# Four attention layers: turned scores ahead of scores in each half step, a first pair of batches by itself, one empty step, loads in another order

## The chip, the cores and the metric

The kernel runs on one core of one Trainium2 chip, in a single launch. The metric is the device time in microseconds of that core, taken over several executions; one more execution is profiled. Its engines are TensorE (PE, with PEld for its weight loads), VectorE (DVE), ScalarE (ACT), GpSimd (POOL) and SyncE (SP), which here only issues DMAs.

## The reference

Four layers of cross attention run one after the other on x of 8 batches x 128 tokens x 128 features, with a context of the same shape. Each has 16 heads.

```python
# L0: heads of 8; a padding mask on the keys; then LayerNorm with gamma, beta
x = LN(x + softmax(q(x) k(ctx) / sqrt(8) + mask) v(ctx) wo + bo)
# L1: heads of 64; RMS norm of x ahead, no scale
x = x + softmax(q(rms(x)) k(ctx)) v(ctx) wo
# L2: block of three
x = x + self_attn(LN(x))      # heads of 8, causal, blocks of 64 dropped by a router
x = x + cross_attn(LN(x), ctx)  # heads of 8, biases
x = x + relu(LN(x) f1 + b) f2 + b   # 512 hidden
# L3: heads of 8, with biases; LayerNorm with gamma, beta at the end
x = LN(x + softmax(q(x) k(ctx) / sqrt(8)) v(ctx) wo + bo)
```

## The kernel before, in words

**Items and steps.** Attention with heads of 8 is done four times over 8 batches: L0, L2 (the self attention), LC (the cross attention of the same block) and L3. That makes 32 items n = 0 to 31, one batch of one layer each. L1, with heads of 64, has a loop of its own (`pe_l1`, `act_l1`, `dve_l1`) between items 7 and 8, and fills about 94 to 202 us. The other items go through a software pipeline of steps s, one item entering per step (`pe_attn`, `act_attn`, `dve_attn`, `pool_attn`). `at(s)` (L200) gives the item of a step. Between LC and L3 there are `HOLES` = 2 steps (24 and 25) into which no item enters, since L3 needs the result of the feed-forward layer, which is itself computed in steps 22 to 30 between attention work. So item 24 enters at step 26, and the last at step 33.

**A step.** It has two halves, for heads with even and odd number of a pair. In half 0 of step s TensorE does, in `pe_scores` (L288): the scores S of item s, queries on the partitions, into banks 0 and 1 (L294); the turned scores T of item s-2 in its second half, keys on the partitions, into banks 4 and 5 (L302); the causal matmuls of L2 (L306, L311); the transpose of the split maxima of item s-1 (`pe_mT`, L326); and the max rows (L320), which add the negative row maximum to the turned scores. Then come the extras of the step (`even(s)`), the transposes `pe_back` (L353) and the output projection `pe_z` (L362). In half 1 it does S of item s for banks 2 and 3, T of item s-1 for its first half, the max rows, `pe_onT` (L358), the extras `odd(s)` and `pe_V` (L345). The instructions of an engine run in the order written, each behind its waits.

**The chain of an item.** S -> VectorE's max of each half (`dve_max`, L465) -> GpSimd splits the 16 maxima into three bf16 parts (`pool_split`, L443 to L448) -> transpose on TensorE, bank 3 -> ScalarE copies it (`act_mrow`, L387) -> T and max rows -> ScalarE's exp (`act_exp`, L393), straight from the turned scores -> V on TensorE -> `act_osum` (L400) -> back -> `dve_norm` (L481, L485) -> onT -> z -> `dve_z` (L493). S of the next item needs its banks free: they are free when max has read them, and when whatever an extra has put there since has been read. `FREED` and `S_ready` hold these waits; the waits for the data of a pair of batches are there too (`data_of_S`).

**Stacks.** Scores are computed to full precision by splitting q and k into three bf16 parts: p0 by ScalarE (`act_p0`, L620), the rest by VectorE (`dve_rest`, L639; L0's k first by `dve_raw`, L599, which applies the mask), p1 by ScalarE (`act_p1`, L647), p2 by VectorE or GpSimd (`any_p2`, L651). DMAs stack the parts into `qs`, `ks0`, `ks1` (`stack_dma`, L663): six for q and six for k of a group of batches, three with p0 and p1, p2 behind. They are issued by SyncE in one order for all layers, except the first q pair of L0, which ScalarE issues. L0's mask goes as three bf16 parts through `up`, a transpose and `kaug` into rows of `ks0`.

**Other work between.** L1's V products for all batches (`pe_v1`, 16 chunks of 512 columns, L705, copied by ScalarE, L710) and the transposes of its weights (`pe_a1`) are extras of L0's steps; `free` waits until max has read the bank. Extras of the later steps: turns of the normalised x (`pe_turn`, L564, copied by `act_turn`, L569) under the names T1, T2, TC, TF, T3, projections (`pe_proj`, L578), V of a layer (`pe_v`, L672), the feed-forward layer (`pe_f1` L927, `pe_f2` L950, `dve_ff` L958). In L3's query part of step s = 24, 26, 28, 30: projection in the even half (bank 2, second half), p0 there, the rest at the end of VectorE's even half, p1 in ScalarE's odd half, p2 on VectorE at step s+1, scores at step s+2.

**The loads.** SyncE issues at the start the first weights, the context in two halves and the mask in two halves, then waits for ks0's zeros (one memset of 128 x 4096 on VectorE, L1465, ahead of everything else on that engine), then the stacks of L0, and only then x, the row vectors `wrow` and the large weights (L988 to L992). `pool_resid` (L523) of L0 adds a bias to x; it stands in GpSimd's queue at step 2, behind split(1) and vpad and ahead of split(2) (L1048).

## Time and profile before

| | us |
|---|---|
| median of 3 executions | 412.18 |
| lowest, highest | 406.12, 413.94 |
| the profiled execution | 406.76 |
| its span, first to last instruction | 405.0 |
| PE, DVE, ACT, POOL busy | 318.9, 248.4, 213.3, 98.8 |
| mean granted TensorE clock, 1 is full speed | 0.928 |

The profile gives times in us from the start of the span. In a line of the timeline the first number is the start, the second the time until the end of the group, then engine, line, operation, output<-input, shape and the number of instructions; in brackets the idle time of the engine before it and what ended it. SPq and ACTq are DMA issues. A window's line gives its length, then for each engine the busy time and in brackets the instructions, then the granted TensorE clock, the share of the DMA engines' time and GB/s.

### The profile page before, as it was taken

What the parts mean: (1) busy time and instruction counts of PE and PEld (TensorE: products, weight loads), DVE (VectorE), ACT (ScalarE), POOL (GpSimd) and SP (SyncE); (2) the same over time, 40 slices, a digit from 0 to 9 for tenths busy, and PEclk for the clock granted to TensorE, in tenths of its full rate; (3) what the DMA queues carried; (4) which work ended last, traced back from release to release, by engine and by line L of the source; (5) the groups of instructions that cost most, each with busy time, mean ns of one, the idle gap of its engine ahead of it and who ended that gap; (6) DMA issues with size and microseconds to landing.
All of it is one profiled execution on the core that took longest, in us unless ns stands there. A gap on an engine that the chain in (4) does not pass through costs nothing.

```text
span 405.0 us, 10131 instructions
## 1 busy us (share of the span) xinstructions
PE 318.9 (79%) x4045; PEld 225.1 (56%) x4045; DVE 248.4 (61%) x482; ACT 213.3 (53%) x457; POOL 98.8 (24%) x268
## 2 busy tenths in 40 slices
PE   5378099898899999798777986886887977797882
PEld 2134055676687778667654543564555664575551
DVE  6445026844997565658656675678757555446864
ACT  1536046676676786678534543445555542335560
POOL 6011323330020001003238213322423321312311
PEclk9979659999999999999999998999989996679998
DMA  6343920000000000002311132202321011010000
GB/s 228 94 116 92 346 104 4 2 3 0 2 2 3 0 2 0 2 2 73 85 41 42 45 99 62 73 21 59 85 82 34 2 41 32 8 34 28 23 28 26
DMA packets 26068, 20.49 MB, mean 51 GB/s; under 512 B 3182, under 2 KB 24566, under 8 KB 25766
## 3 DMA queue, kind: packets, MB, share of 16 engines
q1 hardware_dynamic: 24566, 18.27, 15.1%
q10 hardware_dynamic: 1456, 1.58, 1.1%
q8 instruction: 32, 0.52, 0.5%
q14 instruction: 14, 0.11, 0.1%
HBM read 6.63 MB, written 0.52 MB: 18 GB/s over the span
## 4 chain that ended last, share of the span: by engine, by line
PE 48%; ACT 16%; DVE 14%; issue 9%; POOL 4%; SPq 3%; DMA 3%; ACTq 1%; POOLq 0%; DVEq 0%
ACT probs L832 5%; PE psum L294 4%; PE psum L345 4%; PE psum L320 4%; PE psum L705 4%; PE psum L756 4%; PE psum L731 3%; PE psum L790 3%; SPq L663 3%; ACT probs L840 3%; PE psum L302 3%; PE psum L927 3%; PE psum L950 2%; DVE maxs L465 2%; PE psum L767 2%
## 5 line engine op out<-in xcount | busy, mean ns | idle before, releaser
L465 DVE TENSOR_REDUCE maxs<-psum 128x8 f32<-128x1024 f32 x64 | 77.7, 1216 | 49.0 <-PE psum L294 34.5
L393 ACT ACTIVATE probs<-psum 128x1024 f32<-128x1024 f32 x64 | 65.5, 1023 | 48.5 <-PE psum L320 46.7
L294 PE MATMUL psum<-ks,qs 64*128 64x128 bf16 x512 | 27.2, 229 | 37.1 <-DVE rest L639 10.1
L294 PEld LDWEIGHTS psum<-ks,qs 64*128 64x128 bf16 x512 | 16.7, 98 | 54.4 <-issue 49.6
L345 PE MATMUL psum<-probs,vpad 128*32 128x128 f32 x1024 | 37.0, 288 | 0.0
L832 ACT ACTIVATE probs<-psum,maxs 128x128 f32<-128x128 f32 x128 | 34.8, 391 | 0.5 <-DVE maxs L880 0.5
L345 PEld LDWEIGHTS psum<-probs,vpad 128*32 128x32 f32 x1024 | 27.8, 115 | 13.1 <-issue 9.5
L387 ACT COPY mrow<-psum 128x128 bf16<-128x128 bf16 x32 | 8.5, 265 | 46.4 <-PE psum L326 43.1
L536 POOL TENSOR_SCALAR rstd<-stats 128x2 f32<-128x2 f32 (+1 forms) x19 | 5.2, 273 | 111.4 <-DVE stats L501 111.2
L443 POOL CAST mp<-maxs 128x16 bf16<-128x16 f32 x32 | 6.9, 215 | 93.3 <-DVE maxs L465 92.6
L302 PE MATMUL psum<-qs,ks 64*128 64x128 bf16 x512 | 26.7, 223 | 2.5 <-ACT probs L393 2.5
L880 DVE TENSOR_REDUCE maxs<-psum 128x8 f32<-128x1024 f32 x16 | 19.5, 1221 | 13.7 <-PE psum L756 13.7
L890 DVE TENSOR_REDUCE mres<-probs 128x8 f32<-128x1024 f32 x16 | 19.4, 1215 | 12.3 <-ACT probs L832 12.3
L320 PE MATMUL psum<-mrow,sel 32*128 32x128 bf16 x512 | 26.6, 225 | 0.0
L481 DVE RECIPROCAL rsum<-psum 128x16 f32<-128x16 f32 x32 | 8.1, 255 | 28.8 <-PE psum L353 28.6
L302 PEld LDWEIGHTS psum<-qs,ks 64*128 64x128 bf16 x512 | 17.9, 98 | 5.3 <-ACT probs L393 4.3
L705 PE MATMUL psum<-wmat,ctxT 128*128 128x512 f32 x32 | 20.2, 734 | 0.9 <-DVE maxs L465 0.9
L320 PEld LDWEIGHTS psum<-mrow,sel 32*128 32x128 bf16 x512 | 15.1, 96 | 10.0 <-issue 5.7
L840 ACT COPY probs<-psum 128x1024 f32<-128x1024 f32 x16 | 16.7, 1042 | 7.0 <-PE psum L767 7.0
L782 PE MATMUL psum<-probs,v1all 128*64 128x128 f32 x256 | 17.5, 279 | 3.3 <-ACT probs L840 2.9
L400 ACT COPY osum<-psum 128x256 f32<-128x256 f32 x32 | 12.0, 375 | 15.1 <-PE psum L345 14.4
L894 DVE TENSOR_TENSOR probs<-probs,mres 128x1024 f32<-128x1024 f32 x16 | 19.6, 1225 | 0.6
(159 smaller groups left out, 663.1 us busy)
## 6 DMA issues: line engine op xcount, KB each, us to landing
qs<-part_q SPq DMA_DIRECT2D x78, 64.0 KB, 2.0
ks<-part_k SPq DMA_DIRECT2D x30, 128.0 KB, 2.4
ks<-part_k SPq DMA_DIRECT2D x36, 64.0 KB, 2.0
wmat<-in_wmat SPq DMA_DIRECT2D x1, 1856.0 KB, 11.5
wmat<-in_wmat SPq DMA_DIRECT2D x1, 1024.0 KB, 7.3
qs<-part_q SPq DMA_DIRECT2D x6, 128.0 KB, 2.4
wrow<-in_wrow SPq DMA_DIRECT2D x1, 704.0 KB, 5.0
ctxT<-in_ctxt SPq DMA_DIRECT2D x2, 256.0 KB, 5.4
```

The source lines that it names most:

```text
L294: s_mm = e.matmul(bank(2 * half + r)[:, bt(c)], qs[rows, i, bt(b)], ks[L.slot][rows, i, bt(b)], start=(c == 0), stop=L is not L2, skip_gro ...
L302: e.matmul(bank(4 + r)[:, bt(c)], ks[M.slot][rows, i, bt(b)], qs[rows, i, bt(b)], start=(c == 0), stop=False, skip_group_check=True)
L320: mm = e.matmul(bank(4 + a)[:, bt(i)], sel[rg(j), i, :], mrow[rg(j), m % 2, :], start=False, stop=True, skip_group_check=True)
L345: mm = e.matmul(o_bank(n)[rg(c), bt(half)], vpad[:, n % 2, 4 * half + c, G * a:G * a + G], pt, start=(a == 0), stop=(a == 1), skip_group_c ...
L393: e.activation(probs_of(n, half), bank(4, 2), ACT.Exp, scale=layer(n).scale)\
L465: e.tensor_reduce(maxs[:, n % 2, 8 * half:8 * half + 8], bank(2 * half, 2).rearrange("p (h k) -> p h k", k=P), AX.X, ALU.max, negate=True)\
L705: e.matmul(bank(to), ctxT[:, bt(c // 2)], mat("v1")[:, c % 2 * 512:(c % 2 + 1) * 512], start=True, stop=True).then_inc(L1("v_mm"), 1)
L832: ins = e.activation(probs[:, half, bt(s)], bank(2 * half, 2)[:, bt(s)], ACT.Exp, bias=maxs[:, b % 2, 8 * half + s:8 * half + s + 1])
L840: e.copy(pT[:, half, :], bank(4, 2)).then_inc(L1("pT_out"), 1)
L880: e.tensor_reduce(maxs[:, b % 2, 8 * half:8 * half + 8], bank(2 * half, 2).rearrange("p (h k) -> p h k", k=P), AX.X, ALU.max, negate=True)\
L890: e.tensor_reduce(sums, p8, AX.X, ALU.add).then_inc(L1("sum"), 1)
L894: e.tensor_tensor(p8, p8, rec.unsqueeze(2).broadcast_to([P, 8, P]), ALU.mult).then_inc(L1("norm"), 1)
```

## The change

- `HOLES` is 1: item 24 enters at step 25, and everything behind is one step earlier (steps end at 36, outputs at 31, 33, 35, 37, GpSimd's rstd at 30 to 36).
- `pe_scores` puts T and the max rows of its item ahead of S of the other item, in each half. The transpose of the split maxima comes behind both. ScalarE's `act_mrow` comes behind the exp of the second half.
- The projections of L0 are done for batches 0 and 1 first, then 2 and 3, then 4 to 7. The loads of context, mask and x are cut at 2 batches, not 4.
- ks0's zeros are made by three engines: GpSimd a quarter behind qs's, ScalarE a quarter (an activation with scale 0), VectorE a half behind the parts of the mask. kaug is copied by VectorE, not ScalarE, and stacked by one DMA of 128 rows, not three of 16.
- ScalarE does p0 and p1 of the first pair and then issues all six q transfers in a row. V of L0 for batches 4 to 7 moves from step 1 to ahead of step 0; one v1 chunk fewer is made ahead of step 0, and step 2 has two in its odd half.
- x and wrow are issued behind the q stack of batches 2 and 3, ahead of the stacks of batches 4 to 7. L0's `pool_resid` is at step 3.
- `rest` gets a whole buffer for k.
- End of L1: the turn and the projections of T2's batches 4 and 5 go behind the scores of item 8, their p0 and rest behind the end of L1, their p2 behind GpSimd's split at step 9. T2's first turn is one place later.
- LC's p1 and p2 of q go to the head of the step on their engines. L3's p1 goes to ScalarE's even half and its p2 to the end of VectorE's even half of the same step; L3's projection takes the first half of bank 2 and TF's turn the second half of bank 3, in front of the transpose of the maxima.

```diff
-HOLES = 2
+HOLES = 1
...
-        V1_EVEN = {1: (4,), 2: (7,), 3: (9,), 4: (11,), 5: (13,), 6: (15,)}
-        V1_ODD = {0: (2, 3), 1: (5, 6), 2: (8,), 3: (10,), 4: (12,), 5: (14,)}
-        freed(0, 1, sem("v_out_L1"), 2)
+        V1_EVEN = {1: (3,), 2: (6,), 3: (9,), 4: (11,), 5: (13,), 6: (15,)}
+        V1_ODD = {0: (1, 2), 1: (4, 5), 2: (7, 8), 3: (10,), 4: (12,), 5: (14,)}
+        freed(0, 1, sem("v_out_L1"), 1)
...
-        def pe_scores(e, n, half, m, mhalf, turned=None):
-
-            if n is not None:
-                L, b = layer(n), n % B
-                S_ready(e, n, half)
-                for c, r, rows, i in heads(half):
-                    s_mm = e.matmul(bank(2 * half + r)[:, bt(c)], qs[rows, i, bt(b)], ks[L.slot][rows, i, bt(b)],
-                                    start=(c == 0), stop=L is not L2, skip_group_check=True)
-                if L is not L2:
-                    s_mm.then_inc(sem("S_mm"), 1)
+        def pe_scores(e, n, half, m, mhalf):
+
             if m is not None:
                 M, b = layer(m), m % B
                 T_ready(e, m, mhalf)
                 for c, r, rows, i in heads(mhalf):
                     e.matmul(bank(4 + r)[:, bt(c)], ks[M.slot][rows, i, bt(b)], qs[rows, i, bt(b)],
                              start=(c == 0), stop=False, skip_group_check=True)
-            if n is not None and L is L2:
-                for j in (2 * half, 2 * half + 1):
-                    s_mm = e.matmul(bank(j), identB[:, :], causal[:, 0, :].unsqueeze(1).broadcast_to([P, 4, P]),
-                                    start=False, stop=True, skip_group_check=True)
-                s_mm.then_inc(sem("S_mm"), 1)
-            if m is not None and M is L2 and mhalf:
-                for a in range(2):
-                    e.matmul(bank(4 + a), causal[:, 0, :], identB[:, :].unsqueeze(1).broadcast_to([P, 4, P]),
-                             start=False, stop=False, skip_group_check=True)
-            if turned is not None:
-                pe_mT(e, turned)
-            if m is not None:
+                if M is L2 and mhalf:
+                    for a in range(2):
+                        e.matmul(bank(4 + a), causal[:, 0, :], identB[:, :].unsqueeze(1).broadcast_to([P, 4, P]),
+                                 start=False, stop=False, skip_group_check=True)
                 e.wait_ge(sem("mT_read"), m + 1)
                 for i in range(4):
                     for a in range(2):
@@ -320,6 +305,17 @@
                         mm = e.matmul(bank(4 + a)[:, bt(i)], sel[rg(j), i, :], mrow[rg(j), m % 2, :],
                                       start=False, stop=True, skip_group_check=True)
                 mm.then_inc(sem("T_mm"), 1)
+            if n is not None:
+                L, b = layer(n), n % B
+                S_ready(e, n, half)
+                for c, r, rows, i in heads(half):
+                    s_mm = e.matmul(bank(2 * half + r)[:, bt(c)], qs[rows, i, bt(b)], ks[L.slot][rows, i, bt(b)],
+                                    start=(c == 0), stop=L is not L2, skip_group_check=True)
+                if L is L2:
+                    for j in (2 * half, 2 * half + 1):
+                        s_mm = e.matmul(bank(j), identB[:, :], causal[:, 0, :].unsqueeze(1).broadcast_to([P, 4, P]),
+                                        start=False, stop=True, skip_group_check=True)
+                s_mm.then_inc(sem("S_mm"), 1)
...
-        def pe_attn(e, steps, lo, hi, even, odd):
+        def pe_attn(e, steps, lo, hi, even, odd, ahead=lambda s: None):
             for s in steps:
                 n, n1, n2 = at(s, lo, hi), at(s - 1, lo, hi), at(s - 2, lo, hi)
                 n3, n4 = at(s - 3, lo, hi), at(s - 4, lo, hi)
-                pe_scores(e, n, 0, n2, 1, n1)
+                pe_scores(e, n, 0, n2, 1)
+                ahead(s)
+                if n1 is not None:
+                    pe_mT(e, n1)
...
-        def act_attn(e, steps, lo, hi, even, odd):
+        def act_attn(e, steps, lo, hi, even, odd, first=lambda s, half: None):
             for s in steps:
                 n1, n2, n3 = at(s - 1, lo, hi), at(s - 2, lo, hi), at(s - 3, lo, hi)
                 if n3 is not None:
                     act_osum(e, n3)
+                first(s, 0)
+                if n2 is not None:
+                    act_exp(e, n2, 1)
                 if n1 is not None:
                     act_mrow(e, n1)
-                if n2 is not None:
-                    act_exp(e, n2, 1)
                 even(s)
...
-            e.dma_start(ctxT[:, 0:HALF], ctxt_d[:, 0:HALF]).then_inc(sem("in_ctx0"), 16)
-            e.dma_start(maskbc[:, 0:HALF], mask_d[0:HALF].partition_broadcast(P)).then_inc(sem("in_mask0"), 16)
-            e.dma_start(ctxT[:, HALF:T], ctxt_d[:, HALF:T]).then_inc(sem("in_ctx1"), 16)
-            e.dma_start(maskbc[:, HALF:T], mask_d[HALF:T].partition_broadcast(P)).then_inc(sem("in_mask1"), 16)
-            e.wait_ge(sem("ks0_zero"), 1)
-            stack_dma(e, L0, "k", 0, 2, 0)
-            stack_dma(e, L0, "k", 0, 2, 1)
+            e.dma_start(ctxT[:, 0:PAIR], ctxt_d[:, 0:PAIR]).then_inc(sem("in_ctx0"), 16)
+            e.dma_start(maskbc[:, 0:PAIR], mask_d[0:PAIR].partition_broadcast(P)).then_inc(sem("in_mask0"), 16)
+            e.dma_start(ctxT[:, PAIR:T], ctxt_d[:, PAIR:T]).then_inc(sem("in_ctx1"), 16)
+            e.dma_start(maskbc[:, PAIR:T], mask_d[PAIR:T].partition_broadcast(P)).then_inc(sem("in_mask1"), 16)
+            e.wait_ge(sem("ks0_zero"), 3)
+            stack_up(e, L0, "k", 0, 2)
             e.wait_ge(sem("kaug_out"), 1)
-            for k in range(3):
-                e.dma_start(ks0[8 * k + ROW_SLOT::HD, :, :], kaug[G // 2 * k:G // 2 * k + G // 2, :])\
-                 .then_inc(sem("kaug_in"), 16)
-            stack_dma(e, L0, "k", 0, 2, 2)
+            e.dma_start(ks0[ROW_SLOT::8, :, :], kaug[:, :]).then_inc(sem("kaug_in"), 16)
             stack_up(e, L0, "k", 2, 2)
             stack_up(e, L0, "q", 2, 2)
+            e.dma_start(x[:, :, :], x_d).then_inc(sem("in_x"), 16)
+            e.dma_start(wrow[:, :], wrow_d.partition_broadcast(P)).then_inc(sem("in_rows"), 16)
             stack_up(e, L0, "k", 4, 4)
             stack_up(e, L0, "q", 4, 4)
             e.dma_start(wcol[:, :], wcol_d).then_inc(sem("in_cols"), 16)
...
+            e.memset(wide_f32(ks0, 3), 0.0).then_inc(sem("ks0_zero"), 1)
...
-                if s == 2:
+                if s == 3:
                     e.wait_ge(sem("in_rows"), 16)
...
-                if (b, place) == (7, 0):
-                    e.wait_ge(*L2.v_done("v_out", 0))
-                    pe_turn(e, "T2", 4, 2, 7)
                 if (b, place) == (7, 2):
                     e.wait_ge(sem("masks"), 7)
                     pe_scores(e, B, 0, None, 0)
+                    e.wait_ge(*L2.v_done("v_out", 0))
+                    pe_turn(e, "T2", 4, 2, 7)
+                if (b, place) == (7, 4):
+                    pe_scores(e, B, 1, None, 0)
                     e.wait_ge(sem("xnT_T2"), 2)
                     pe_proj(e, L2, "k", 4, 2, 7)
                     pe_proj(e, L2, "q", 4, 2, 7, PAIR)
-                if (b, place) == (7, 4):
-                    pe_scores(e, B, 1, None, 0)
...
-                if 22 <= s <= 28 and s % 2 == 0:
-                    free(e, s, 0)
-                    if s == 24:
-                        e.wait_ge(sem("ff_read"), 1)
-                    pe_turn(e, "TF", s - 22, 2, 2)
                 if 24 <= s <= 30 and s % 2 == 0:
                     p = (s - 24) // 2
                     free(e, s, 0)
                     e.wait_ge(sem("ff_read"), p + 1)
                     e.wait_ge(sem("xnT_T3"), p + 1)
-                    pe_proj(e, L3, "q", 2 * p, 2, 2, PAIR)
+                    pe_proj(e, L3, "q", 2 * p, 2, 2)
 
...
+            def ahead2(s):
+                if 22 <= s <= 28 and s % 2 == 0:
+                    free(e, s, 0)
+                    pe_turn(e, "TF", s - 22, 2, 3, c0=2)
...
-            act_p0(e, L0, "k", 0, 4)
-            act_p0(e, L0, "q", 0, 4, 1)
+            e.wait_ge(sem("identF"), 1)
+            e.activation(wide_f32(ks0, 2), identF[:, 0:1].broadcast_to([P, T]), ACT.Identity, scale=0.0)\
+             .then_inc(sem("ks0_zero"), 1)
+            act_p0(e, L0, "k", 0, 2)
+            act_p0(e, L0, "q", 0, 2, 1)
+            act_p1(e, L0, "k", 0, 2)
+            act_p1(e, L0, "q", 0, 2)
             e.wait_ge(sem("qs_one"), 1)
             stack_dma(e, L0, "q", 0, 2, 0)
-            act_p1(e, L0, "k", 0, 2)
-            act_p1(e, L0, "q", 0, 2)
             stack_dma(e, L0, "q", 0, 2, 1)
-            e.wait_ge(sem("kaug_mm"), 1)
-            e.copy(kaug[:, :], bank(3).bitcast(BF16)).then_inc(sem("kaug_out"), 1)
             stack_dma(e, L0, "q", 0, 2, 2)
+            act_p0(e, L0, "k", 2, 2)
+            act_p0(e, L0, "q", 2, 2, 6)
             act_p1(e, L0, "k", 2, 2)
             act_p1(e, L0, "q", 2, 2)
-            act_v(e, L0, 0, 4)
             act_p0(e, L0, "k", 4, 4)
-            act_p0(e, L0, "q", 4, 4, 6)
-            act_v1(e, 0, 7)
-            act_v1(e, 1, 2)
+            act_p0(e, L0, "q", 4, 4, 7)
+            act_v1(e, 0, 2)
+            act_v(e, L0, 0, 5)
+            act_v(e, L0, 1, 6)
...
+            def first2(s, half):
+                if half == 0 and 15 <= s <= 21 and s % 2:
+                    act_p1(e, LC, "q", s - 15, 2)
+                if half and 24 <= s <= 30 and s % 2 == 0:
+                    act_p1(e, L3, "q", s - 24, 2)
...
+            e.memset(ks0[:, 0:4, :].rearrange("p c t -> p (c t)").bitcast(F32), 0.0).then_inc(sem("ks0_zero"), 1)
+            dve_raw(e, 0, 2, 0)
+            dve_rest(e, L0, "k", 0, 2)
+            dve_rest(e, L0, "q", 0, 2, 1)
             any_p2(e, L0, "k", 0, 2)
             any_p2(e, L0, "q", 0, 2)
+            e.wait_ge(sem("kaug_mm"), 1)
+            e.tensor_copy(kaug[:, :], bank(3).bitcast(BF16)).then_inc(sem("kaug_out"), 1)
+            dve_raw(e, 2, 2, 5)
...
+            def first2(s):
+                if 15 <= s <= 21 and s % 2:
+                    any_p2(e, LC, "q", s - 15, 2)
+
             def end_of_even(s):
                 if 24 <= s <= 30 and s % 2 == 0:
-                    e.wait_ge(sem("xnT_TF"), min(4, (s - 22) // 2 + 1))
-                    dve_rest(e, L3, "q", s - 24, 2, 2, PAIR)
-
-            for s in range(9, 39):
-                dve_attn(e, [s], B, N_ITEM, even2, odd2, end_of_even)
+                    dve_rest(e, L3, "q", s - 24, 2, 2)
+                    any_p2(e, L3, "q", s - 24, 2)
+
+            for s in range(9, 38):
+                dve_attn(e, [s], B, N_ITEM, even2, odd2, first2, end_of_even)
```

## Rows read from the trace of the kernel before

**Rows 1.** Windows of the span; each engine busy, its instructions, then clock, DMA, GB/s
```profile
39.60:59.30 19.70, 9.45 (x95) 5.03 (x92) 3.00 (x4) 4.02 (x7) 5.17 (x12) 0.58 0.65 240
59.30:83.10 23.80, 22.13 (x376) 15.32 (x372) 17.95 (x45) 16.36 (x30) 10.03 (x30) 0.99 0.01 3
247.00:307.40 60.40, 48.03 (x762) 32.38 (x764) 42.04 (x81) 30.21 (x57) 17.30 (x53) 0.92 0.25 69
320.20:387.80 67.60, 54.80 (x792) 39.79 (x788) 39.23 (x83) 30.36 (x61) 17.45 (x56) 0.85 0.10 27
326.80:332.00 5.20, 4.63 (x75) 3.88 (x71) 1.88 (x7) 1.94 (x4) 0.60 (x2) 1.00 0.11 29
332.00:342.80 10.80, 6.44 (x39) 4.11 (x35) 6.29 (x12) 2.70 (x7) 2.77 (x8) 0.71 0.11 30
...
202.00:214.00 12.00, 9.74 (x119) 6.40 (x113) 5.55 (x11) 3.86 (x9) 4.95 (x11) 1.00 0.19 51
```

**Rows 2.** Waits between 32 and 62 us: total us, times, longest
```profile
POOL resid L523 <- DMA wrow<-in_wrow: 13.7, 1, 13.7
```

**Rows 3.** Timeline, 32 to 62 us
```profile
36.63 3.82 SPq L663 DMA_DIRECT2D qs<-part_q  x6
...
39.65 0.40 PE L294 MATMUL psum<-ks,qs 64*128 64x128 bf16 x8
...
41.63 0.43 SPq L990 DMA_DIRECT2D wrow<-in_wrow  x1
...
46.73 2.48 POOL L523 TENSOR_TENSOR resid<-x,wrow 128x512 f32<-128x512 f32 x2 [13.66 <-DMA wrow<-in_wrow]
...
59.27 0.61 PE L294 MATMUL psum<-ks,qs 64*128 64x128 bf16 x8
```

**Rows 4.** Timeline, 0 to 32 us
```profile
1.86 3.51 POOL L1032 MEMSET qs<- 128x4096 f32 x1
...
5.56 1.38 POOL L1034 MEMSET vpad<- 128x1536 f32 x1
5.83 1.50 DVE L1478 CAST probs<-mu 128x128 bf16<-128x128 f32 x1
...
7.05 0.20 POOL L1037 MEMSET causal<- 128x128 bf16 x1
...
7.58 0.23 DVE L1482 CAST probs<-mu 128x128 bf16<-128x128 f32 x1
...
8.19 0.68 DVE L599 TENSOR_TENSOR rest<-psum,xn 128x512 f32<-128x512 f32 x1
...
8.96 1.28 ACT L620 ACT_TABLE_LOAD   x1 [8.96 <-DVE rest L599]
...
20.78 1.04 PE L294 MATMUL psum<-ks,qs 64*128 64x128 bf16 x16 [6.61 <-DMA ks<-part_k]
...
22.75 3.81 SPq L663 DMA_DIRECT2D qs<-part_q  x6
```

**Rows 5.** Groups of instructions by line, 200 to 405 us
```profile
L294 PE MATMUL psum<-ks,qs 64*128 64x128 bf16 x384 | 20.2, 226 | 25.4 <-DVE rest L639 10.1 <-ACT xnT L569 7.7 <-DMA qs<-part_q 2.6
L302 PE MATMUL psum<-qs,ks 64*128 64x128 bf16 x384 | 19.9, 223 | 2.5 <-ACT probs L393 2.5
```

**Rows 6.** Timeline of TensorE, 297 to 298 us
```profile
297.25 0.40 PE L302 MATMUL psum<-qs,ks 64*128 64x128 bf16 x8
...
297.91 0.33 PE L358 MATMUL psum<-identF,onorm 128*128 128x128 f32 x1
```

**Rows 7.** Timeline, 320 to 377 us; last, a row of the page's DMA issues
```profile
321.99 0.66 PE L578 MATMUL psum<-xnT,wmat 128*64 128x256 f32 x4
...
322.69 0.47 ACT L620 ACTIVATE part_q<-psum,bcol 128x256 bf16<-128x256 f32 x1
...
370.29 6.13 SPq L663 DMA_DIRECT2D qs<-part_q  x6
...
qs<-part_q SPq DMA_DIRECT2D x78, 64.0 KB, 2.0
```

158 lines of the change are left out of this document (75 added, 83 removed).

## The prediction

> **What bounds the kernel now.** I read first the busy times by stretch [rows 1], then the waits inside the stretch that stood out [rows 2], then the timeline there [rows 3], the timeline of the beginning [rows 4], and last what TensorE waits for before a group of scores [rows 5, 6] and the way from the L3 query projection to the stacks [rows 7]. The reader is to see four things.
>
> First, TensorE is busy 22.1 of 23.8 us in steps 4 to 7 (59.3 to 83.1), and only 9.5 of 19.7 us in step 3 (39.6 to 59.3), where its granted clock is 0.58 [rows 1]. That step is a hole: GpSimd sits 13.7 us before `pool_resid` until `wrow` has landed, and TensorE with it, since the split of the maxima stands behind the residual in GpSimd's queue [rows 2, 3]. Second, the first scores start at 20.78, released by the last k stack; until then only projections ran [rows 4]. Third, from step 10 on TensorE is not the bound: it is busy 48.0 of 60.4 us (247 to 307.4), and it sits idle before 28 of the 48 groups of scores (counted in the waits by line), 25.4 us in all, mostly until a bank of PSUM is read out (rest 10.1, xnT 7.7) [rows 1, 5]. Behind each of these scores stand the turned scores, which could run. Fourth, between 93.8 and 202 lies L1, which is hardly touched.
>
> **The change part by part.** The profiled execution took 406.76 us, 405.0 of it the span; terms are against that.
>
> *Loads in another order (x and wrow, and `pool_resid` at step 3).* In before, SyncE issues x and then wrow (41.63) behind all twelve (4,4) stack transfers, and they are there at 46.73 [rows 3]; the residual then takes 2.48 us. In after both are issued right behind the q stack of (2,2), whose last issue was at 22.75 + 3.81 = 26.6 in before. 5.1 us from wrow's issue to its use makes some 32, and step 3 starts at 39.65 before [rows 3, 4]. The transfers moved past are the (4,4) stacks: their p0 parts queue behind 1.2 MB, some 5 us, but their last parts wait for VectorE's p2 of step 2 anyway and are not later; the last issue ended at 36.63 + 3.82 = 40.45, with 2.0 to land [rows 7] 42.5, and step 4 would start at about 45.6 [rows 3]. At step 3 the 2.48 us of residual lie between vpad(2) and split(3); max(3,1) ends some 4.5 us into the step, so the maxima hide them with one memset (0.95). If this cover went, 2 us would be lost once. Step 3 took 59.27 - 39.65 = 19.62; steps 4 to 7 take 23.8 / 4 = 5.95. Gain **13.7** (11 to 14).
>
> *First pair by itself.* Half-size operations: VectorE's raw product 0.68 becomes some 0.4, and so on down the chain, twice on ScalarE and three times on VectorE, together about 1.3; the table load of 1.28 leaves the path, since ScalarE now zeroes a quarter of ks0 before the data come [rows 4]; kaug takes one issue for three, some 1.2 less by 0.64 each [rows 3]. ks0's memset goes from the head of VectorE's queue to behind the mask's parts and is halved; GpSimd's of the same size takes 3.51, so 1.75 are left. Against it stand three things. ScalarE issues all six q transfers (0.64 each, 3.8 us [rows 3]) before p0 of (2,2), so (2,2) and (4,4) come later on it, and scores (0,1) now wait for the copy of v1 chunk 0 behind them. And the cast of the mask part: it took 1.50 us where the same cast later took 0.23; it started at 5.83 and ended at 7.33, when GpSimd's run of memsets (5.56 to 7.25) had ended [rows 4]. In after the mask arrives at about 2.7, in the middle of the 3.51 us memset, and GpSimd's run is a quarter of that longer (to 8.1): if the cast waits for all of it, the mask's parts end at 9.1, the memset at 10.9 and the raw product at 11.3, later than the 8.87 of now. ScalarE then has 10.5 us in its queue before scores (0,1) are free (p0 and p1 of the pair 1.8, the issues 3.8, p0 and p1 of (2,2) with their rests in between 1.9, p0 of (4,4) behind VectorE 2.4, the v1 copy 0.6): 21.8, and their maxima end within 0.3 of now; with what goes behind them step 1 starts some 0.8 earlier. If the cast doesn't wait, VectorE is 4 us earlier, ScalarE's issues take back a little, and step 1 starts 4.6 earlier. I take **1** for the start, near the waiting end because of the row of 1.50; the ends are a loss of 1 and a gain of 4.6.
>
> The row shows more than one instruction's hold: the cast, begun beside the vpad memset (5.56 to 6.94), ended 0.39 us after it, with the short ones that followed [rows 4]. The Trainium skill (SBUF — State Buffer, "Who interferes with whom") says that VectorE's cast in a two-port mode and any GpSimd instruction exclude each other on a shared pair of ports, and that whichever starts first has it for its one instruction. By that rule the cast would get in behind the first memset, at 5.4 (1.86 + 3.51) and not at 8.1, and the start would gain 1 + 2.7 = 3.7; by the row it gains 1. No row shows a cast that got in between two memsets.
>
> In steps 1 and 2 a V product (1.11) leaves step 1 and half a v1 pair (0.9) enters step 2: nothing.
>
> *Turned scores first.* Turned scores and max rows together hold TensorE for 0.66 (297.25 to 297.91) [rows 6]. Where scores waited, up to 0.66 now goes under the wait: 28 waits of 0.9 on average [rows 5] give at most 18 us from step 10 on, and less where one is shorter; about 15. What limits it: where VectorE or ScalarE is what the scores wait for, the step gains only the 0.2 by which exp starts earlier, and scores that did not wait come 0.66 later, and with them max (1.22), split (0.95), the transpose and the max rows of the next step. So I take **6** of 15, between -2 (loss) and 11; p1 and p2 of LC's queries, now at the head of ScalarE's and VectorE's step, take away part of the waits for q stacks and are in it. In steps 3 to 8 TensorE idles 0.33 before each group behind a v1 copy and is otherwise full, so I take **3** (0 to 5).
>
> *End of L1.* T2's turn and the (4,2) projections go behind the scores of batch 8, so L1's last two turns no longer stand behind them, and max(8,1) no longer waits for two rests; the projections then stand before scores (9,0). GpSimd loses the two p2 in front of split(8), which the transpose waits for. TensorE is idle 2.3 of the 12.0 us of 202 to 214 [rows 1], and that is the upper end, since none of its work goes. I take **1.5**, since both waits named lie there; -0.5 is the lower end, the projections (about 1 us) half uncovered. The (4,2) stacks come some 5 us later and are needed at step 12, 20 us on.
>
> *One empty step.* The step 326.8 to 332 (5.2 us) goes, but it holds 4.6 us of TensorE's work [rows 1], which moves into its neighbours; of these, step 26 (332 to 342.8) has 4.4 us of idle TensorE, and the pure last steps become one fewer. Without a new wait this would be 5. The new wait: L3's queries had two steps from projection to scores, and have one. From the projection's start (321.99) to the end of p0 (323.16) it is 1.2 us, six issues take 3.8 [rows 3] and the landing 2.0: 7.0 [rows 7]. In a step of 7.5 the projection starts some 1.8 in and the scores stand 0.4 behind the next step's start: 6.1 after it. So some 1 us is waited at steps 25, 27, 29, 31, with f2 and the transposes behind them in TensorE's queue, 4 in all; VectorE also waits for p1 before p2 and its max, but no longer for xnT. Net **1** (-5 to 5).
>
> Sum: 13.7 + 1 + 6 + 3 + 1.5 + 1 = 26.2, so 380.6 at the profiled level. The three timed executions had a median of 412.18, 5.4 above the profiled one; their spread (406.1 to 413.9) is mostly not tied to a stage I can name, and fewer idle stretches should leave less of it. I put half, 2.7, on top: **383**.
>
> **The rivals.**
> 1. *The order gives nothing*: turned scores in front only delay max, split and the max rows by what they fill. For: S, max, split, transpose, max rows are one chain through every step; against: 25.4 us of idle before scores [rows 5]. Without 9 us: 392.
> 2. *The start gains nearly all*: the cast gets the ports as soon as GpSimd's first memset has ended, and the beginning is 3.7 to 4.6 shorter, not 1. For: a cast beside a later GpSimd instruction took 0.23; against: the 1.50. 380. By the rule of the Trainium skill quoted above it is this case.
> 3. *L3's queries come late*: six issues took 6.13 once instead of 3.8 [rows 7], which makes 9.3 of 7.0 and four waits of 3.3 instead of 1; with what stands behind them 10 us more, 393.
> 4. *The load stall stays*, moved to step 3's split, because x and wrow land only beside the stacks: 14 lost, 397.
 It decides once over 76% of that stretch (29 of 38) is at the low level; before, 332 to 342.8 was at 0.71, and it rose again.
>
> **How the numbers follow.** Forecast 0.58, rivals 0.17, 0.13, 0.06, 0.03, 0.03. The range 371 to 398 takes in the ends of the order (11 instead of 6, 5 instead of 3) and the start on one side, rivals 1, 3 and 4 on the other. A measurement tells about 2% (8.2 us) from no change: faster means under 404. Every case but the last is under that; with 0.04 for several ends together, 0.93 faster, 0.04 within, 0.03 slower.
>
> **What would show it.** Right: no wait for wrow on GpSimd, step 3 near 6 us at full clock, a granted clock above 0.928 on the whole; idle before scores from step 10 well under 25.4; idle before turned scores (2.5 now [rows 5]) up by less than that fell. The cast near 5 us if held. DMA waits of 1 to 1.5 before scores at steps 25 to 31. Wrong: steps 4 to 7 still at 5.95, steps 14 to 21 still at 7.5, a hole anywhere between 15 and 60, or 10 us of waits for qs stacks.

## The result and the profile after

The changed kernel took 365.09 us, the median of four executions (362.0 to 367.26), beside 410.75 (406.12 to 413.94) for the kernel before on the same chip: a ratio of 0.892 (95% interval 0.880 to 0.903). Forecast were 383 us and a range of 371 to 398: the direction was right, but the time lies 6 us below the range, a gain of 45.7 us where 29 were forecast. Ratios and their intervals leave out executions more than 1.5% above the fastest of their kernel, medians do not. The profiled execution took 362.0 us, 360.3 of it the span, at a granted clock of 0.98 (before 0.928).

Below, "exp 8.0" is the start of ScalarE's exp of item 8's first half, "exp 7.1" of item 7's second half, and so on; every item has both in every kernel, so a distance between two exps compares a stretch over kernels. The windows of the changed kernel that answer to [rows 1]; the columns are PE, PEld, DVE, ACT, POOL busy with their instructions, then clock, DMA, GB/s:

```profile
36.70:42.50 5.80, 5.80 (x106) 3.32 (x99) 3.00 (x4) 3.92 (x8) 4.27 (x8) 1.00 0.67 190
42.50:65.40 22.90, 22.56 (x389) 15.01 (x388) 17.66 (x44) 16.78 (x31) 10.11 (x31) 1.00 0.28 114
191.19:348.39 157.20, 137.07 (x2240) 92.38 (x2237) 114.26 (x227) 86.45 (x167) 57.14 (x162) 0.98 0.19 52
```

The same stretch as the last row, exp 8.0 to exp 31.1, in the kernel before:

```profile
214.10:393.13 179.03, 144.58 (x2230) 99.86 (x2229) 114.56 (x225) 87.20 (x167) 53.46 (x157) 0.91 0.16 44
```

Step 3 is no hole any more: TensorE is busy in all of the 5.80 us of its window, where it was busy 9.5 of 19.7 [rows 1]. In steps 4 to 7 it is idle 0.3 us, where it was 1.7. The surprise is the last pair of rows: 157.20 us instead of 179.03, so 21.8 us came from where 7 were forecast. The profiled execution was the fastest of its four; in the other profile of the same kernel (`after_again`, below) this stretch took 161.5 us at a clock of 0.95, so two executions of one kernel can differ by some 4 us in such a stretch. TensorE's idle time fell from 34.5 to 20.1 us (14.3), and its busy time from 144.6 to 137.1 (7.5), with the same work and a clock of 0.98 instead of 0.91.

The residual [rows 3] no longer waits. The beginning, in the timeline of the changed kernel:

```profile
1.86 3.51 POOL L1033 MEMSET qs<- 128x4096 f32 x1
3.12 5.12 DVE L1480 CAST probs<-mu 128x128 bf16<-128x128 f32 x1
...
7.95 0.20 POOL L1039 MEMSET causal<- 128x128 bf16 x1
...
11.22 0.36 DVE L599 TENSOR_TENSOR rest_k<-psum,xn 128x256 f32<-128x256 f32 x1
...
21.67 0.61 PE L312 MATMUL psum<-ks,qs 64*128 64x128 bf16 x8 [1.62 <-ACT v1all L714]
...
37.51 2.49 POOL L525 TENSOR_TENSOR resid<-x,wrow 128x512 f32<-128x512 f32 x2
```

The cast of the mask was held until 8.24 (8.1 forecast), the raw product came at 11.22 (11.3), scores (0,1) at 21.67 (21.8), behind the copy of v1.

The groups of TensorE's instructions that answer to [rows 5], 180 to 361 us: L312 are the scores, L295 the turned scores, L354 the transposes in `pe_onT`; behind the bar busy and mean, then the idle time before them. The last line is that of the same transposes in the kernel before, 200 to 405 us.

```profile
L312 PE MATMUL psum<-ks,qs 64*128 64x128 bf16 x384 | 19.3, 220 | 11.4 <-DMA qs<-part_q 6.9 <-DVE rest_q L643 2.7 <-DVE vall L685 0.8
L295 PE MATMUL psum<-qs,ks 64*128 64x128 bf16 x384 | 19.3, 220 | 0.5 <-ACT probs L392 0.4
L354 PE MATMUL psum<-identF,onorm 128*128 128x128 f32 x24 | 8.0, 332 | 7.0 <-DVE onorm L486 7.0
...
L358 PE MATMUL psum<-identF,onorm 128*128 128x128 f32 x24 | 8.1, 336 | 4.1 <-DVE onorm L485 4.0
```

Idle before scores fell from 25.4 to 11.4, and what is left is mostly DMA. The wait before the transposes of the normalised output grew from 4.1 to 7.0.

### The profile page after: what moved, and what is told of

Read it like the earlier page. It is cut to its first block, busy times and chain, and to the rows that moved or that the text cites. A ratio compares the mean times of both kernels' runs of the same rounds, so it can differ in the third digit from the quotient of the medians.

```text
span 360.3 us, 10155 instructions
## 1 busy us (share of the span) xinstructions
PE 307.4 (85%) x4053; PEld 215.9 (60%) x4053; DVE 250.1 (69%) x486; ACT 212.6 (59%) x459; POOL 100.3 (28%) x269
## 4 chain that ended last, share of the span: by engine, by line
PE 44%; DVE 19%; ACT 12%; issue 7%; POOL 6%; SPq 5%; DMA 5%; ACTq 1%; POOLq 0%
SPq L667 5%; PE psum L341 5%; ACT probs L836 5%; DMA qs<-part_q 4%; PE psum L794 4%; DVE maxs L466 4%; PE psum L709 4%; PE psum L760 4%; PE psum L312 4%; PE psum L735 3%; ACT probs L844 3%; PE psum L955 3%; PE psum L295 3%; PE psum L305 3%; PE psum L771 2%
## 5 line engine op out<-in xcount | busy, mean ns | idle before, releaser
L312 PE MATMUL psum<-ks,qs 64*128 64x128 bf16 x512 | 25.9, 221 | 14.2 <-DMA qs<-part_q 6.9
L341 PE MATMUL psum<-probs,vpad 128*32 128x128 f32 x1024 | 35.0, 278 | 0.0
L341 PEld LDWEIGHTS psum<-probs,vpad 128*32 128x32 f32 x1024 | 26.4, 110 | 12.1 <-issue 8.1
L312 PEld LDWEIGHTS psum<-ks,qs 64*128 64x128 bf16 x512 | 15.1, 95 | 23.5 <-issue 9.5
L885 DVE TENSOR_REDUCE maxs<-psum 128x8 f32<-128x1024 f32 x16 | 19.5, 1220 | 11.7 <-PE psum L760 11.7
L295 PE MATMUL psum<-qs,ks 64*128 64x128 bf16 x512 | 25.6, 220 | 0.5 <-ACT probs L392 0.4
L305 PE MATMUL psum<-mrow,sel 32*128 32x128 bf16 x512 | 25.5, 218 | 0.1
L295 PEld LDWEIGHTS psum<-qs,ks 64*128 64x128 bf16 x512 | 14.5, 95 | 13.4 <-issue 7.7
L399 ACT COPY osum<-psum 128x256 f32<-128x256 f32 x32 | 12.0, 375 | 14.3 <-PE psum L341 14.0
L305 PEld LDWEIGHTS psum<-mrow,sel 32*128 32x128 bf16 x512 | 14.5, 93 | 9.5 <-issue 3.6
L540 POOL TENSOR_TENSOR rstd<-rstd,small 128x2 f32<-128x2 f32 (+1 forms) x23 | 17.9, 780 | 1.9
L786 PEld LDWEIGHTS psum<-probs,v1all 128*64 128x64 f32 x256 | 13.7, 136 | 7.1 <-ACT probs L844 5.9
L354 PE MATMUL psum<-identF,onorm 128*128 128x128 f32 x32 | 10.6, 332 | 8.6 <-DVE onorm L486 8.6
```

Of the source, the lines that this page charges most:

```text
L295: e.matmul(bank(4 + r)[:, bt(c)], ks[M.slot][rows, i, bt(b)], qs[rows, i, bt(b)], start=(c == 0), stop=False, skip_group_check=True)
L305: mm = e.matmul(bank(4 + a)[:, bt(i)], sel[rg(j), i, :], mrow[rg(j), m % 2, :], start=False, stop=True, skip_group_check=True)
L312: s_mm = e.matmul(bank(2 * half + r)[:, bt(c)], qs[rows, i, bt(b)], ks[L.slot][rows, i, bt(b)], start=(c == 0), stop=L is not L2, skip_gro ...
L341: mm = e.matmul(o_bank(n)[rg(c), bt(half)], vpad[:, n % 2, 4 * half + c, G * a:G * a + G], pt, start=(a == 0), stop=(a == 1), skip_group_c ...
L786: mm = e.matmul(bank(6)[HD * pp:HD * pp + HD, bt(t)], v1[:, b, h * HD:(h + 1) * HD], pT[:, half, bt(4 * pp + t)], start=True, stop=True)
L885: e.tensor_reduce(maxs[:, b % 2, 8 * half:8 * half + 8], bank(2 * half, 2).rearrange("p (h k) -> p h k", k=P), AX.X, ALU.max, negate=True)\
```

## The experiments

There were twelve runs, in three lots of four, each lot on one chip with the kernel before; `after_again` is the changed kernel a second time, and `v_wait2` is `v_wait` a second time. The medians of the kernel before were 412.7, 409.1 and 411.8 us. The distances between exps in the profiled executions, in us, each worked out from two exp rows of the timeline of one profile (four of the runs are left out):

| stretch (exps) | before | changed | d_loads | d_order | d_three | u_order | u_turn | u_holes | v_wait2 | v_two |
|---|---|---|---|---|---|---|---|---|---|---|
| start to 1.0 | 37.7 | 33.7 | 39.8 | 35.7 | 35.3 | 39.8 | 33.9 | 35.8 | 30.2 | 29.1 |
| 1.0 to 2.1 (steps 2, 3) | 23.0 | 9.5 | 9.1 | 22.1 | 8.6 | 9.9 | 9.5 | 9.5 | 9.5 | 9.5 |
| 2.1 to 7.1 | 30.0 | 29.7 | 30.0 | 29.7 | 29.7 | 30.0 | 29.7 | 29.7 | 29.7 | 29.7 |
| 7.1 to 8.0 (L1) | 123.3 | 118.3 | 124.7 | 123.8 | 120.1 | 119.6 | 121.9 | 118.3 | 118.3 | 118.3 |
| 8.0 to 20.0 | 90.1 | 78.2 | 92.5 | 81.5 | 81.9 | 87.7 | 78.4 | 78.3 | 81.6 | 78.4 |
| 20.0 to 23.1 | 23.4 | 23.2 | 23.1 | 25.0 | 24.4 | 24.7 | 23.2 | 23.1 | 20.7 | 23.2 |
| 23.1 to 24.0 (hole) | 21.0 | 12.8 | 21.1 | 18.0 | 20.4 | 10.2 | 13.1 | 20.4 | 13.2 | 20.2 |
| 24.0 to 31.1 | 44.5 | 43.1 | 46.0 | 40.1 | 40.3 | 49.8 | 44.5 | 37.7 | 44.9 | 37.7 |

### The loads alone (d_loads)

```diff
 # the kernel before
             stack_up(e, L0, "q", 2, 2)
+            e.dma_start(x[:, :, :], x_d).then_inc(sem("in_x"), 16)
+            e.dma_start(wrow[:, :], wrow_d.partition_broadcast(P)).then_inc(sem("in_rows"), 16)
             stack_up(e, L0, "k", 4, 4)
             stack_up(e, L0, "q", 4, 4)
             e.dma_start(wcol[:, :], wcol_d).then_inc(sem("in_cols"), 16)
-            e.dma_start(x[:, :, :], x_d).then_inc(sem("in_x"), 16)
-            e.dma_start(wrow[:, :], wrow_d.partition_broadcast(P)).then_inc(sem("in_rows"), 16)
...
-                if s == 2:
+                if s == 3:
                     e.wait_ge(sem("in_rows"), 16)
```

> The kernel before with one part of the change alone: x and the row vectors issued ahead of the k and q stacks of batches 4 to 7, and L0's residual at step 3. Theory A (the stall is the load and nothing else): 13.5 us faster than before, 397.2, all of it by the exps of item 2, the residual without a wait, steps 3 to 8 as before. Rival B (the stall had also lowered the clock behind it, or other stages have the slack to take part back): under 10 or over 16 us faster.

Measured: 395.62 us, ratio 0.967 (0.953 to 0.980): 13.7 us of 412.7, the middle of an interval of 8 to 19. Its residual, in the timeline, without a wait:

```profile
42.22 2.49 POOL L523 TENSOR_TENSOR resid<-x,wrow 128x512 f32<-128x512 f32 x2
```

The stretch from exp 1.0 to 2.1 is 14.0 us shorter, and steps 4 to 8 are as before. Other stretches are up to 2.4 us longer in this one profile, the slowest of its four executions (399.85 us), whose clock was a little lower (0.921, before 0.928); the medians have the middle of theory A, though their interval alone would leave room for rival B. Theory A holds by the stretch: the stall was the load. The edit holds two things, the earlier issue and the residual one step later, and they were not run apart.

### The order undone in the changed kernel (u_order)

```diff
 # pe_scores and the order in pe_attn as before: S, causal, mT, T's max rows
+                pe_scores(e, n, 0, n2, 1, n1, lambda: ahead(s))
-                pe_scores(e, n, 0, n2, 1)
-                ahead(s)
-                if n1 is not None:
-                    pe_mT(e, n1)
...
+                if n1 is not None:
+                    act_mrow(e, n1)
                 if n2 is not None:
                     act_exp(e, n2, 1)
-                if n1 is not None:
-                    act_mrow(e, n1)
```

> The changed kernel with the order of a half step as before: scores, causal matmuls, transpose of the maxima, then turned scores' max rows; on ScalarE the max rows' copy ahead of exp. All else is the changed kernel's (365.1 us). Theory A (the order itself brought what items 9 to 20 gained, 10.4 us by their exps, and some of what lies behind): 11 to 16 us slower than the changed kernel, 376 to 381, of it 9 to 11 between the exps of items 9 and 20 and under 1 in steps 3 to 8; idle before scores behind L1 back to over 20 us from 11.4. Rival B (LC's p1 and p2 at the head of the step, and the clock, brought half of it): 5 to 7 slower, 370 to 372, idle before scores up by under 6 us. Rival C (the order also carries the gain in the hole before item 24, 8.3 us): 20 or more slower, and the hole between the exps of items 23 and 24 at over 18 us instead of 12.8.

Measured: 384.63 us, ratio 0.941 (0.928 to 0.953), 19.5 us above the changed kernel's 365.1, which ran on another chip. That is more than theory A had and near the time of rival C. Its one profile is 23.3 us longer than that of the changed kernel. The exps 9.0 to 20.0 lie 8.0 us farther apart (9 to 11 expected) and 8.0 to 9.0 1.6; exps 2.1 to 7.1 0.4. What it had left out: the beginning, 6.1 us later at exp 1.0, 1.3 in L1, 1.6 from exp 20.0 to 23.1, and 4.1 us from exp 23.1 to 31.1. Of the 6.1 some 2 are clock (0.55 from 20 to 30 us, where the changed kernel had 0.83; u_holes with the changed kernel's own beginning and a clock of 0.52 there was 2.0 later). Rival C falls by its own sign: the hole was 10.2 us, not over 18. Idle before scores was back, and idle before the transposes for `onorm` was down to 1.5:

```profile
L295 PE MATMUL psum<-ks,qs 64*128 64x128 bf16 x384 | 19.8, 223 | 26.8 <-DMA qs<-part_q 7.4 <-ACT xnT L574 7.4 <-DVE rest_q L646 5.2
```

(L295 is the line of the scores in that kernel.)

### The order alone (d_order)

The same edit, the other way round, in the kernel before.

> The kernel before with one part of the change alone: turned scores, causal matmuls and max rows ahead of the scores in each half step, and exp ahead of the max rows' copy on ScalarE; loads, empty steps, banks and the query path as before. Theory A (the order carries its gain by itself, as the run without it showed between the exps of items 8 and 20): 15 to 20 us faster than before (391 to 396): 1.6 between the exps of items 8 and 9, 3 to 4 from 9 to 13, 4 to 5 from 13 to 20, about 4 from item 23 on, 2 to 4 up to item 1, nothing in steps 3 to 8. Rival B (it needs the other edits: LC's p1 and p2 at the head of the step, TF's turn in another bank): under 9 us faster, over 402.

Measured: 389.99 us, ratio 0.955 (0.949 to 0.961): 18.4 of 409.1 us (16 to 21). Theory A holds in the whole and nearly by its parts: 1.6 between exps 8.0 and 9.0, 3.9 from 9.0 to 13.0, 3.2 from 13.0 to 20.0 (4 to 5 expected), 2.0 up to exp 1.0, 0.9 from 1.0 to 2.1, 0.3 from 2.1 to 7.1. Behind item 20 it is less even (1.7 lost to exp 23.1, with 5.6 us at a clock of 0.70 in it, and 7.5 gained after, where about 4 were expected). First its groups of instructions, then its window from exp 8.0 to 31.1 (L311 are the scores there, L353 the transposes in `pe_onT`):

```profile
L311 PE MATMUL psum<-ks,qs 64*128 64x128 bf16 x384 | 19.7, 223 | 11.6 <-DVE rest L637 5.4 <-DMA qs<-part_q 4.3 <-DVE wmat L937 1.1
L353 PE MATMUL psum<-identF,onorm 128*128 128x128 f32 x24 | 8.2, 341 | 8.3 <-DVE onorm L483 8.3
```

```profile
211.23:375.81 164.58, 140.13 (x2240) 93.68 (x2238) 113.02 (x225) 87.09 (x166) 54.76 (x159) 0.96 0.18 48
```

So the order by itself takes 13.8 us of idle before scores away, and the wait before the transposes grows from 4.1 to 8.3. Over the stretch it is 14.5 us shorter: TensorE's idle time falls by 10.0 (34.5 to 24.5), and its busy time by 4.5, at a clock of 0.96 and not 0.91. That is one profile of each; two profiles of the changed kernel differ by 4.1 in the same busy time. But the clock of the whole span was 0.935 to 0.948 in the four executions of d_order and 0.909 to 0.936 in the seven of the kernel before, so the rise is no accident of the pair.

### Three parts together (d_three)

The kernel before with the loads, the order, and T2's first turn at place (4,4).

> The kernel before with three parts: the loads ahead of the last stacks, the order of the half step, and T2's first turn one place later in L1. Theory A (the three add up, 14 + 17 + 3.6): 375 to 378, and the other edits (first pair by itself, one empty step less, query path of L3, end of L1, banks) are worth the remaining 10 us or so to the changed kernel's 365.1. Rival B (the other edits bring next to nothing): 365 to 369. Rival C (loads and order overlap, since both fill TensorE's idle time in steps 2 and 3): 380 or more.

Measured: 372.12 us, ratio 0.910 (0.904 to 0.916): 37.0 us of 409.1. That is between theory A (375 to 378) and B (365 to 369). The parts measured one by one give 13.7 + 18.4 + 3.6 (the turn, from a profile below) = 35.7, so they add up within the intervals. The rest of the change is worth the remaining 7 us, give or take some 4 (the ratios, 0.910 and 0.891, with their intervals).

### T2's turn (u_turn)

```diff
-                if (b, place) == (4, 4):
+                if (b, place) == (4, 3):
```

(in TensorE's and ScalarE's part of L1)

> The changed kernel with T2's first turn back at the earlier place in L1 (batch 4, place 3), on TensorE and ScalarE. Theory A (the one place brought the 2.1 us that appeared between L1's 9th and 10th turned probabilities): 2.1 us slower, 367.2, all of it there and kept to the end. Rival B (the 2.1 us came from the other edits, or are given back before the end of L1): within 0.5 us of the changed kernel at the exp of item 8.

Measured: 368.37 us, ratio 0.902 (0.892 to 0.913), which can't be told from the changed kernel. The profile can: L1 took 121.9 instead of 118.3, and with the later place it was 118.33 to 118.36 in eight profiles. Timeline of u_turn, then of the changed kernel, at the turn:

```profile
147.39 1.11 DVE L557 TENSOR_SCALAR xn<-x,stats,rstd 128x128 f32<-128x128 f32 x4
148.65 1.09 PE L566 MATMUL psum<-identF,xn 128*128 128x128 f32 x4 [2.27 <-DVE xn L557]
149.78 0.78 ACT L571 ACTIVATE xnT<-psum,wcol 128x512 f32<-128x512 f32 x1 [2.69 <-PE psum L566]
```

```profile
147.21 1.09 PE L786 MATMUL psum<-probs,v1all 128*64 128x128 f32 x16
148.35 0.59 ACT L850 COPY resid<-psum 128x512 f32<-128x512 f32 x1 [1.46 <-PE psum L786]
148.45 0.63 PE L566 MATMUL psum<-identF,xn 128*128 128x128 f32 x4
```

The windows from 149 to 154 us, of u_turn and then of the changed kernel:

```profile
149.00:154.00 5.00, 5.00 (x53) 4.15 (x52) 1.24 (x2) 1.88 (x5) 0.00 (x0) 0.71 0.00 0
149.00:154.00 5.00, 5.00 (x46) 4.67 (x46) 3.60 (x5) 3.50 (x11) 0.00 (x0) 1.00 0.00 0
```

At the earlier place the turn stands in TensorE's queue ahead of a product of 1.09 us and waits 2.27 for VectorE's normalisation; one place later that product runs in the meantime. It is worth 3.6 us in this profile, more than the 2.1 expected, and the prediction had no term for it. Some 1.5 of the 3.6 goes with the clock: TensorE was busy 107.4 us in L1 instead of 105.9. The same wait of 2.27 stands in the kernel before, d_loads and d_order; in the two latter the clock fell there too (0.986 over L1, as in u_turn), in the kernel before it did not (1.00), and it never did in the ten profiles with the later place. The difference without the fall is 2.0: L1 took 123.35 before and 120.07 in d_three, and 1.3 of these 3.3 are the order's (u_order).

### The empty step (u_holes, v_two)

```diff
-HOLES = 1
+HOLES = 2
```

(with the ranges of the steps, the last normalisation and the outputs one step later)

> The changed kernel with two empty steps again (item 24 enters at step 26; L0 to LC and L3's query path unchanged, the final normalisation one step later). Theory A (the step was worth nearly all of what items 23 to 31 gained, since it held mostly waiting, and the slow clock in it made it dearer): 8 to 11 us slower than the changed kernel's 365.1, 373 to 376, exps of items 23 to 24 some 20 us apart instead of 12.8. Rival B (its work only moves; most of the gain of that stretch came from the order and from TF's turn in another bank): 1 to 4 slower, 366 to 369, and the distance under 17. Rival C (a step of its own length, at full clock): 5.2 slower, 370.

Measured: 366.24 us, ratio 0.898 (0.886 to 0.909), 1.2 us above the changed kernel (2.4 by the ratios, whose intervals overlap): rival B by the time. The distance of exps 23.1 and 24.0 was not under 17 as rival B had it, but 20.4, as theory A had. The pair with the earlier mask (below) settles it, with the same beginning and five rounds on one chip:

> The same with two empty steps again before item 24. Theory A (of the 5.2 us of the step nearly all was work that only moved, and the shorter hole is paid back behind item 26, where the clock is lower): 0 to 2 us slower than with one empty step; hole 7 to 8 us longer, exps of items 26 to 31 some 5 us closer. Rival B (the step was worth what the hole lost, 7.6 us): 6 or more slower. Rival C (the full clock behind item 26 outweighs it): faster.

Measured: 360.54 us, ratio 0.880 (0.874 to 0.885), beside 360.94, 0.881 (0.876 to 0.887), for v_wait2, the same kernel with one empty step: no difference, theory A. The windows exps 23.1 to 24.0, 24.0 to 26.0 and 26.0 to 31.1 of v_wait2, then of v_two:

```profile
290.03:303.21 13.18, 9.13 (x110) 7.13 (x112) 7.23 (x17) 3.44 (x9) 3.37 (x9) 0.87 0.04 11
303.21:315.74 12.53, 11.06 (x171) 8.03 (x172) 8.66 (x16) 7.39 (x16) 4.46 (x14) 1.00 0.10 28
315.74:348.13 32.39, 28.73 (x502) 20.64 (x502) 21.67 (x48) 17.31 (x35) 8.35 (x30) 0.89 0.11 31
```

```profile
288.13:308.33 20.20, 15.27 (x137) 11.91 (x139) 10.31 (x23) 4.53 (x11) 3.37 (x9) 0.75 0.09 24
308.33:320.38 12.05, 10.83 (x168) 7.74 (x167) 8.20 (x15) 7.23 (x13) 4.51 (x14) 1.00 0.13 34
320.38:345.99 25.61, 22.16 (x478) 15.62 (x476) 19.84 (x45) 16.49 (x32) 8.29 (x30) 1.00 0.09 24
```

The hole is 7.0 us shorter with one empty step, and the last stretch 6.8 longer: 24 of TensorE's instructions have moved there, and its clock was 0.89 instead of 1.00. A look at the hole alone, the 8.3 us by which exp 24.0 gained on exp 23.1, would have credited the step with nearly all of it.

### The mask and GpSimd's memsets (v_gap, v_wait, v_wait2)

```diff
+            e.wait_ge(sem("up"), 3)            # v_wait, v_wait2
             e.memset(qs[:, :, :].rearrange("p c t -> p (c t)").bitcast(F32), TWO_ONES).then_inc(sem("qs_one"), 1)
+            e.wait_ge(sem("qs_one"), 1)        # v_gap
             e.memset(wide_f32(ks0, 3), 0.0).then_inc(sem("ks0_zero"), 1)
```

> The changed kernel with one wait more: GpSimd waits for the end of its own first memset (3.51 us) before it starts the next, so that there is a gap between the two. Theory A (a cast that waits gets in as soon as GpSimd has nothing running): the cast ends at 5.4 to 5.8 instead of 8.24, the parts that follow it are held by the second run of memsets or get by. Rival B (the gap is too short or the hold is not of that kind): the cast ends near 8.2 as now.

Measured: 362.2 us (two executions), ratio 0.887 (0.881 to 0.893); exp 0.0 came at 26.2 instead of 29.2. Its timeline:

```profile
2.89 2.56 DVE L1481 CAST probs<-mu 128x128 bf16<-128x128 f32 x1
5.42 0.95 POOL L1035 MEMSET ks<- 128x1024 f32 x1
...
5.69 0.77 DVE L1485 CAST probs<-mu 128x128 bf16<-128x128 f32 x1
6.32 0.39 POOL L1036 MEMSET mp<- 128x256 bf16 x1
...
6.70 1.41 DVE L1489 CAST probs<-mu 128x128 bf16<-128x128 f32 x1
```

The cast ends at 5.45, in the gap behind the 3.51 us memset: theory A. The two casts behind it got in at the end of the memset that was running (6.46, 8.11), without a gap of their own.

> The changed kernel with one wait more: GpSimd's run of memsets begins only when the three parts of the mask are written. Theory A (the run of memsets held the 128x128 cast on VectorE for 4.9 us, and that is what the first raw product waited for): cast 0.2 to 0.3, mask parts done near 4.5 instead of 9.2, raw product near 7 to 8 instead of 11.2, first exp 1 to 4 us earlier, 361 to 364. Rival B (the 3.5 us memset now runs beside VectorE's own memset of ks0 and holds that, or qs and ks0 come late for the stacks): raw product not before 10, first exp within 1 us or later, 365 or more.

Measured: 360.94 us, ratio 0.881 (0.874 to 0.888). The mask's parts and the raw product in its timeline:

```profile
3.11 0.23 DVE L1481 CAST probs<-mu 128x128 bf16<-128x128 f32 x1
...
4.33 3.51 POOL L1034 MEMSET qs<- 128x4096 f32 x1 [2.41 <-DVE probs L1489]
...
4.65 1.76 DVE L1491 MEMSET ks<- 128x2048 f32 x1 [0.37 <-issue]
6.71 0.42 DVE L599 TENSOR_TENSOR rest_k<-psum,xn 128x256 f32<-128x256 f32 x1 [0.29 <-DMA xn<-in_mask]
```

Theory A, and a little more than it had: all three casts take 0.23, the raw product comes at 6.7 (7 to 8 expected), and exp 0.0 at 23.9 instead of 29.2. VectorE's own fp32 memset of 1.76 ran beside GpSimd's and was not held. For five rounds beside the changed kernel:

> The kernel in which GpSimd's memsets begin behind the mask's parts, again, beside the changed kernel. Theory A (the 5.3 us gained at the first exp stay, less what a lower clock at items 20 to 21 takes now and then): 3 to 5 us faster than the changed kernel. Rival B (what the start gains is lost at items 20 to 21 every time): under 2 us faster.

> The changed kernel itself, beside the next three on one chip. 363 to 367 us; exps of items 23 and 31 some 56 to 58 us apart, depending on the clock behind item 26.

Measured: 360.94 us (358.44 to 363.14), ratio 0.881 (0.876 to 0.887), for v_wait2, and 365.66 (362.2 to 370.0), ratio 0.891 (0.884 to 0.898), for the changed kernel. The difference of the medians is 4.7 us, that of the ratios 4.0 (theory A had 3 to 5), though the two intervals, each against the kernel before, overlap a little. v_wait2 and v_two are the fastest kernels of this study.

### LC's p1 and p2 (u_lc)

```diff
 # ScalarE and VectorE: from first2(s) back to even2(s)
                 if 15 <= s <= 21 and s % 2:
                     act_p1(e, LC, "q", s - 15, 2)
...
                     any_p2(e, LC, "q", s - 15, 2)
```

> The changed kernel with p1 and p2 of LC's queries back at their place in the middle of the step on ScalarE and VectorE. Theory A (this edit is what separates the changed kernel from the one with loads, order and turn alone between the exps of items 9 and 20, 77.5 against 73.7 us): 3 to 4 us slower than the changed kernel, all of it between items 13 and 20, and the waits of scores for q stacks there longer. Rival B (the stacks come early enough either way, and the difference was the clock): within 1 us of the changed kernel.

Measured: 366.2 us, ratio 0.893 (0.887 to 0.899), beside 0.891 for the changed kernel: rival B. From exp 13.0 to 23.1 it took 70.1 us, the changed kernel 68.5 and, again, 72.1. Its profile does have theory A's sign, 49.2 us from exp 13.0 to 20.0 where the changed kernel had 45.3 and 46.0, but v_wait2, which lacks this edit, shows the same 48.7; in both the clock was 0.93 there, and both get 2 us back up to exp 21.1.

## Why the prediction missed, point by point

**The load stall: right.** 13.7 forecast, 14.0 by the stretch, 13.7 by the ratio. Its step holds as written: the cut is the wait, corrected by when step 4 could start at all.

**The start: right in its mechanism, short in its sum.** 1 forecast, 4.0 measured at exp 1.0. The cast's row and what followed from it were hit to 0.2 us. The term that was missing is the order, which was priced from step 3 on only; by d_order it gives 2.0 of the 4.0 (the distance between exps 0.0 and 1.0 goes from 6.6 to 4.5, and is 4.8 in u_holes, whose clock was 0.52 there). The other 1.9 stand at exp 0.0 already; 1.6 of them appear only from d_three to the changed kernel, so they are the first pair with what goes with it, none of it run alone.

**The cast, by the row and not by the rule.** In the changed kernel it was held through a run of seven memsets, from 3.12 to 8.24. The Trainium skill (SBUF — State Buffer, "Who interferes with whom") gives the pair of ports to whichever starts first for its one instruction; the prediction's estimate by it was 5.4. The trace of the changed kernel doesn't bear this out, and the measurement decides. v_gap agrees with it, in the gap (5.45) and in the two casts behind it, which got in at the end of the memset that was running though the next stood ready. What decides between the two cases is open. The rival "the start gains nearly all" was thus wrong for this kernel, and what it described is what v_wait reaches.

**The order in steps 3 to 8: too high.** 3 forecast, 0.8 measured: 0.4 from d_loads to d_three between exps 1.0 and 2.1, and 0.3 to 0.4 from 2.1 to 7.1 in each kernel with the new order. In steps 4 to 7 it did give 1.1 (exps 2.1 to 6.1 went from 23.34 to 22.25 in d_order), but 0.75 of it was lost again in step 8 (exps 6.1 to 7.1 from 6.68 to 7.43).

**The order from step 10 on: the step that failed.** 6 was taken out of "about 15" and a worked-out upper end of 18; d_order measured 14.5 from exp 8.0 to 31.1, and u_order took 15.2 more there than the changed kernel (10.9 more than its other profile). The mechanism was right, the size was not: the whole order, forecast at 6 + 3, gave 18.4 us (16 to 21) by itself. Two things were wrong in the discount. First, the price of the other side: scores that did not wait come 0.66 later, and this was to cost max, split and the max rows. It cost less: from exp 26.0 to 31.1, at full clock in both, d_order took 25.9 us and the kernel before 26.9. What shows of it is the 0.75 in step 8 and 4.2 us more before the transposes for `onorm`, a wait that was not foreseen. Second, the clock was no part of the term. Of the 14.5 only 10.0 are idle time, more than 6 and still inside the end of 11; the other 4.5 are TensorE's own work at 0.96 instead of 0.91. That less idle time would raise the clock was said for the whole, where 2.7 were put on top for the spread; it had its place here.

**The end of L1: right in size, with a part missing.** 1.5 forecast; from d_three to the changed kernel L1 falls by 1.7. L1 fell by 5.0 in all. The turn of T2 one place later, named in the change and never priced, gave 2.0 of it (3.6 where the clock had fallen behind its wait), and the order 1.3. It is an edit of one digit, in a stretch called "hardly touched".

**The empty step: right.** 1 forecast, -0.4 and 1.2 measured, which can't be told from nothing. The step held TensorE's work, and this came back behind it. The waits for L3's query stacks came to 3.7 us in three waits in the changed kernel (4 in four forecast), so rival 3 was as unlikely as it looked.

**The rest.** Of the 7 us between d_three and the changed kernel, 3.3 lie at the start and the end of L1. LC's p1 and p2 and the empty step are none of the other 3.7 that can be measured; TF's turn in another bank and L3's p1 and p2 in the same step stay as candidates and were not run alone. The 3.7 are also no more than the uncertainty of the 7.

The slower rival asked for a clock at the low level over most of items 24 to 31. The clock did fall to 0.89 to 0.95 behind item 26 with one empty step (0.85 in u_order); that is an estimated 1.4 to 3.2 us (5 to 11% of TensorE's 27.2 to 28.7 us of work there), and not 38.
